# Gate and up of blocks 2 to 7 as seven products of 2x2 block matrices

## The reference

```python
x = fwht(x * SU_ug) / SCALE
x_up = x @ W_up.T * (Wscale_ug[:INTER] * SCALE)
x_gate = x @ W_gate.T * (Wscale_ug[INTER:] * SCALE)
x = jax.nn.silu(x_gate) * x_up
x = fwht(x * SU_dp) / SCALE
x = x @ W_down.T * (Wscale_dp * SCALE)
```

## Time and profile before

| | |
|---|---|
| median of 3 runs | 1306.21 us (1305.66 to 1310.3) |
| the profiled execution | 1306.45 us |
| its span, first to last instruction | 1304.6 us |
| mean granted TensorE clock | 0.979 of 2.4 GHz |
| PE busy / weight loads | 1226.0 us / 584.9 us |
| VectorE / ScalarE / GpSimd busy | 660.7 / 436.0 / 574.7 us |
| moved by DMA | 112.86 MB, mean 87 GB/s |

### The profile page before, as it was taken

One profiled execution on the slowest core, in us unless ns is written; L12 is line 12 of the kernel. 1 busy time (PEld: TensorE's weight loads), 2 busy tenths in 40 slices (PEclk: granted clock), 3 DMA queues, 4 the chain that ended last, 5 costly groups with the idle time before them and its releaser, 6 DMA issues.

```text
span 1304.6 us, 18006 instructions
## 1 busy us (share of the span) xinstructions
PE 1226.0 (94%) x6718; PEld 584.9 (45%) x6718; DVE 660.7 (51%) x1252; ACT 436.0 (33%) x828; POOL 574.7 (44%) x492
## 2 busy tenths in 40 slices
PE   7865879889999999999999999999999999999998
PEld 4552334334444444444444444444444444444444
DVE  2589599555564545544644545454554454451110
ACT  4874665521243023411432134302341143212210
POOL 1462487411575237531764166523753176311210
PEclk9987889999999999999999999999999999999999
DMA  9810144543452344333443345234433343120000
GB/s 322 309 33 1 33 73 87 107 97 65 113 106 59 95 104 106 65 81 90 109 93 73 87 107 106 51 96 104 106 65 81 93 109 82 33 73 9 1 1 32
DMA packets 230904, 112.86 MB, mean 87 GB/s; under 512 B 209400, under 2 KB 210736, under 8 KB 230320
## 3 DMA queue, kind: packets, MB, share of 16 engines
q1 hardware_dynamic: 219632, 77.52, 26.6%
q0 software_dynamic: 10240, 33.56, 9.3%
q10 hardware_dynamic: 960, 0.75, 0.2%
HBM read 52.82 MB, written 9.70 MB: 48 GB/s over the span
## 4 chain that ended last, share of the span: by engine, by line
PE 77%; DVE 9%; POOL 5%; ACT 4%; issue 3%; DMA 2%; SPq 0%; ACTq 0%; DVEq 0%; POOLq 0%
PE bank L1434 24%; PE bank L1435 24%; PE bank L1436 24%; DMA att<-ids_b 1%; POOL p L529 1%; PE bank L1610 1%; DVE wd L689 1%; POOL h_row L556 1%; POOL hid L580 1%; DVE a L1036 1%; PE bank L1429 1%; DVE h L677 1%; ACT sg L1147 1%; PE bank L1660 1%; PE bank L1499 1%
## 5 line engine op out<-in xcount | busy, mean ns | idle before, releaser
L1434 PE MATMUL bank<-xT,wgu 128*128 128x512 f16 x1024 | 391.4, 382 | 4.7 <-DVE a L1036 2.8
L1435 PE MATMUL bank<-xT,wgu 128*128 128x512 f16 x1024 | 391.3, 382 | 0.0
L1436 PE MATMUL bank<-xT,wgu 128*128 128x512 f16 x1024 | 391.0, 382 | 0.0
L580 POOL TENSOR_TENSOR hid<-a,hid 128x512 f16<-128x512 f32 x128 | 174.4, 1362 | 171.5 <-ACT hid L1150 171.3
L1036 DVE SCALAR_TENSOR_TENSOR a<-bank,kap,sg 128x512 f32<-128x512 f32 x128 | 96.0, 750 | 299.5 <-PE bank L1436 225.3
L1434 PE MATMUL bank<-wd,hid 128*128 128x512 f16 x512 | 195.2, 381 | 0.0
L1436 PE MATMUL bank<-wd,hid 128*128 128x512 f16 x512 | 195.1, 381 | 0.0
L1435 PE MATMUL bank<-wd,hid 128*128 128x512 f16 x512 | 195.1, 381 | 0.0
L1434 PEld LDWEIGHTS bank<-xT,wgu 128*128 128x128 f16 x1024 | 101.1, 99 | 125.1 <-issue 6.3
L1436 PEld LDWEIGHTS bank<-xT,wgu 128*128 128x128 f16 x1024 | 100.8, 98 | 123.0 <-issue 3.8
L1435 PEld LDWEIGHTS bank<-xT,wgu 128*128 128x128 f16 x1024 | 100.7, 98 | 118.7 <-issue 2.8
(11 more groups left out here) (223 smaller groups left out, 1470.0 us busy)
## 6 DMA issues: line engine op xcount, KB each, us to landing
out<-a SPq DMA_DIRECT2D x24, 256.0 KB
wgu<-in_L_ffn_W_gate SPq DMA_DIRECT2D x4, 1024.0 KB, 14.8
wgu<-in_L_ffn_W_up SPq DMA_DIRECT2D x4, 1024.0 KB, 15.0
wd<-in_L_ffn_W_down SPq DMA_DIRECT2D x4, 1024.0 KB, 15.8
out<-h_row SPq DMA_DIRECT2D x8, 256.0 KB
hid<-att_table,ids_p POOLq DMA_INDIRECT x72, 3.6
xT<-in_L_tok_proj_weight SPq DMA_DIRECT2D x1, 1024.0 KB, 8.6
p<-in_L_attn_Wq SPq DMA_DIRECT2D x1, 1024.0 KB, 12.0
```

What stands on the lines that cost most here:

```text
L580: nc.gpsimd.tensor_tensor(hid[:, 1, s, :], a32[:, :], hid[:, 0, s, :], ALU.subtract)\
L1434: mm(dst, w[0], v[0], start=first, stop=False)
L1435: mm(dst, w[0], v[1], start=False, stop=False)
L1436: return mm(dst, w[1], v[0], start=False, stop=final)
```

## The change

For one tile `f` gate and up together are a 2x2 block matrix (two halves of 256 rows of input each for gate and up) and the tokens a 2x2 block matrix too (input halves by halves of 256 tokens). Before, all eight block products are made. After, blocks 2 to 7 use seven (Winograd's form), each of six matmuls of 256 columns. Four of them need sums of weights (`S1` to `S4`) and sums of inputs (`T1` to `T4`).

The chain of partial results: bank `CHAIN[f % 2]` accumulates four products one after the other, and ScalarE copies the bank after each (`see`) before PE adds the next. `PAIR[f % 2]` takes the other three. VectorE adds copies and banks to gate and up (`upper`, `diagonal`); SiLU and the multiplication then read SBUF (`gated`) and run one slot later than the products.

The sums of weights are made during block 1 (`prep`: two additions of 512 and four of 256 columns on VectorE; a copy of 1,024 on ScalarE; a subtraction of 1,024 on GpSimd; 16 times), stored to DRAM (`products`, 917,504 bytes a tile) beside the plain quarters (`direct_store`, 32 DMAs). From then on six tiles are held in the SBUF room of `wgu`, and ScalarE issues a load of one tile per slot. The input's sums are made in slots 28 and 30 (`x_high_corner`, `x_low_corner`). The row copies wait for `stored` inside `head_high` now instead of at the loop's end. The diff's core:

```diff
 
+PREP_AT = (0, 2, 4, 5, 7, 8, 10, 11, 13, 14, 16, 18, 20, 22, 24, 26)
+FIRST_LOADS_AT = {21: (0,), 23: (3,), 28: (4, 5), 30: (1, 2)}
+HELD = 6
+HELD_AT = (18432, 11264, 14848, 22016, 25600, 29184)
+A11, A12, A22, S1, S2, S3, S4 = range(7)
...
                     fetch(b + 1, s)
-                    pair(b, s)
-            for s in range(SLOTS):
-                feed(NB - 1, s)
+                    product(b + 1, s)
+                    if s:
+                        feed(b, s - 1)
+                    attend(b + 1, s)
+            for s in range(1, SLOTS):
+                feed(NB - 1, s - 1)
 
...
+            def x_low_corner(n, m):
+                i, c = 4 * n + m, slice((m % 2) * P, (m % 2) * P + P)
+                mixed = PICK[1][:, :].rearrange("p (q k t) -> p q k t", q=2, k=2)
+                dve.wait_ge(S["xThi_done"], turned_high(n, m))
+                if m < 2:
+                    nc.vector.tensor_tensor(x_corner[:, 0:2, 1, :, c], mixed, x_corner[:, 0:2, 0, :, c], ALU.subtract)\
+                        .then_inc(S["xT_done"], 1)
+                    return
+                t = 6 * n + 3 * (m - 2) - 12
+                nc.vector.tensor_tensor(x_t[:, 0:256], PICK[1][:, 0:256], x_kept[m - 2][:, 0:256], ALU.subtract)\
+                    .then_inc(S["xt_done"], 1)
+                nc.vector.tensor_tensor(x_corner[:, B22, 1, :, c], mixed[:, 1, :, :], x_corner[:, B22, 0, :, c], ALU.subtract)
+                dve.wait_ge(S["xt_done"], t + 1)
+                nc.vector.tensor_tensor(x_t[:, 256:512], PICK[1][:, 256:512], x_t[:, 0:256], ALU.subtract)\
+                    .then_inc(S["xt_done"], 1)
+                dve.wait_ge(S["xt_done"], t + 2)
+                nc.vector.tensor_tensor(x_t[:, 512:1024].rearrange("p (a c) -> p a c", a=2),
+                                        x_kept[m - 2].rearrange("p (a c) -> p a c", a=2),
+                                        x_t[:, 256:512].rearrange("p (a c) -> p a c", a=1).broadcast_to([P, 2, 256]),
+                                        ALU.subtract).then_inc(S["xt_done"], 1)
+                dve.wait_ge(S["xThi_done"], turned_high(n, m) + 1)
+                nc.vector.tensor_tensor(x_sums[:, :, 1, :, c], x_t.rearrange("p (q k t) -> p q k t", q=4, k=2),
+                                        x_sums[:, :, 0, :, c], ALU.subtract).then_inc(S["xT_done"], 1)
...
+            def prep(f):
+                g, i = f // 4, f % 4
+                whole, sums, _ = prep_home(f)
+                if f == 0:
+                    dve.wait_ge(S["y_ready"], 4)
+                if f == 3:
+                    dve.wait_ge(S["direct_stored"], 512)
+                if f:
+                    dve.wait_ge(S["st_scaled"], staged_low(f - 1))
+                for j in range(2):
+                    w = wgu[:, 2 * g + j, i, :, :, :].rearrange("p l k f -> p l (k f)")
+                    last = nc.vector.tensor_tensor(whole[:, 512 * j:512 * j + 512], w[:, 0, :], w[:, 1, :], ALU.add)
+                link(last)
+                a11, a12, a21, a22 = [whole[:, 256 * j:256 * j + 256] for j in range(4)]
+                s1, s2, s3, s4 = [sums[:, 256 * j:256 * j + 256] for j in range(4)]
+                if f:
+                    dve.wait_ge(S["st_low"], staged_low(f - 1))
+                nc.vector.tensor_tensor(s3, a21, a11, ALU.subtract)
+                link(nc.vector.tensor_tensor(s1, a21, a22, ALU.add))
+                link(nc.vector.tensor_tensor(s2, s1, a11, ALU.subtract))
+                nc.vector.tensor_tensor(s4, a12, s2, ALU.subtract).then_inc(S["st_scaled"], 1)
...
+            def diagonal(b, f):
+                dve.wait_ge(S["chain_ready"], chain(b, f, 3))
+                dve.wait_ge(S["seen"], chain(b, f, 3))
+                nc.vector.tensor_tensor(corners[f % 2].rearrange("p (a c) -> p a c", a=4)[:, 0:4:3, :],
+                                        seen13[f % 2].rearrange("p (a c) -> p a c", a=2),
+                                        PAIR[f % 2][:, :].rearrange("p (a c) -> p a c", a=2), ALU.add).then_inc(S["corner_done"], 1)
+
+            def upper(b, f):
+                dve.wait_ge(S["p3_ready"], feeding(b, f) + 1)
+                nc.vector.tensor_tensor(corners[f % 2][:, 256:512], seen2[f % 2], PAIR[f % 2][:, 256:512], ALU.add)\
+                    .then_inc(S["corner_done"], 1)
+
+            def gated(b, f):
+                dve.wait_ge(S["silu_done"], FT * b + f + 1)
+                dve.wait_ge(S["seen"], chain(b, f, 4))
+                dve.wait_ge(S["corner_done"], 2 * FT * b + (2 * f - 4 * FT + 1))
+                dve.wait_ge(S["al_done"], FT * b + f - 1)
+                nc.vector.scalar_tensor_tensor(a_pair[f % 2], corners[f % 2][:, 512:1024], kap[:, f:f + 1], sg[:, :],
+                                               ALU.mult, ALU.mult).then_inc(S["a_done"], 1)
+
             def row_of(n, m):
...
+            def corner_slot(b, s, attending):
+                if 0 < s <= FT:
+                    upper(b, s - 1)
+                if attending:
                     if s == 0:
                         ids(b + 1)
                     else:
                         product(b + 1, s)
-                    feed(b, s, UP[s % 2])
+                if s < FT:
+                    diagonal(b, s)
+                if 0 < s <= FT:
+                    gated(b, s - 1)
+
...
 
+            def x_high_corner(n, m):
+                i, c = 4 * n + m, slice((m % 2) * P, (m % 2) * P + P)
+                mixed = PICK[1][:, :].rearrange("p (q k t) -> p q k t", q=2, k=2)
+                act.wait_ge(S["xhada_ready"], i + 1)
+                if m == 0 and isinstance(n, int):
+                    act.wait_ge(S["up_ready"], FT * n)
+                    act.wait_ge(S["sums_stored"], 160)
+                elif m == 0:
+                    act.wait_ge(S["p3_ready"], feeding(n, 0))
+                if m < 2:
+                    copy(x_corner[:, 0:2, 0, :, c], mixed)
+                    copy(x_kept[m], PICK[1][:, :]).then_inc(S["xThi_done"], 1)
+                    return
+                copy(x_corner[:, B22, 0, :, c], mixed[:, 1, :, :]).then_inc(S["xThi_done"], 1)
+                act.wait_ge(S["xt_done"], 6 * n + 3 * (m - 2) - 9)
+                copy(x_sums[:, :, 0, :, c], x_t.rearrange("p (q k t) -> p q k t", q=4, k=2)).then_inc(S["xThi_done"], 1)
...
+            def see(dst, b, f, number):
+                act.wait_ge(S["chain_ready"], chain(b, f, number))
+                copy(dst, CHAIN[f % 2][:, 0:256]).then_inc(S["seen"], 1)
+
+            def corner_slot(b, s, loading):
+                if s == 0:
+                    see(seen13[0][:, 0:256], b, 0, 1)
+                if s < FT:
+                    see(seen2[s % 2], b, s, 2)
+                    see(seen13[s % 2][:, 256:512], b, s, 3)
+                if 0 < s <= FT:
+                    f = s - 1
+                    act.wait_ge(S["corner_done"], 2 * FT * b + (2 * f - 4 * FT + 2))
+                    nc.scalar.activation(sg[:, :], corners[f % 2][:, 0:512], ACT.Silu, scale=sc[:, f:f + 1]).then_inc(S["silu_done"], 1)
+                    if f + HELD < FT:
+                        held_load(f % HELD, f + HELD)
+                    elif loading:
+                        held_load(f % HELD, f % HELD)
+                if s + 1 < FT:
+                    see(seen13[(s + 1) % 2][:, 0:256], b, s + 1, 1)
+                if s < FT:
+                    see(corners[s % 2][:, 512:768], b, s, 4)
+
+            def corner_high(b, s):
+                if 0 < s <= FT:
+                    f = s - 1
+                    if f == FT - 4 and not (isinstance(b, int) and b == NB - 1):
+                        for way in range(1, 5):
+                            act.wait_ge(S[f"pt_land{way}"], 48 * b)
+                    act.wait_ge(S["a_done"], FT * b + f + 1)
+                    copy(hid[:, 0, f, :], a_pair[f % 2]).then_inc(S["ah_done"], 1)
 
             def feed_high(b, s):
                 if s < FT:
...
-                    if s:
-                        product(b + 1, s)
-                    feed(b, s, GATE[s % 2])
-                    feed_high(b, s)
-                    if s == 0:
-                        product(b + 1, s)
+                    corner_slot(b, s, True)
+                    product(b + 1, s)
+                    corner_high(b, s)
                     attend(b + 1, s)
-                act.wait_ge(S["y_ready"], 4 * b + 4)
-                act.wait_ge(S["stored"], 64 * b + 64)
             for s in range(SLOTS):
-                feed(NB - 1, s, GATE[s % 2])
-                feed_high(NB - 1, s)
...
+            def quarter_product(dst, f, w, x, begin, final):
+                for k in range(2):
+                    last = split_mm(dst, [held[f % HELD][:, l, w, k, :] for l in range(2)], [XQ[x][:, l, k, :] for l in range(2)],
+                                    begin and k == 0, final and k == 1, skip_group_check=not begin)
+                return last
+
+            def p1(b, f):
+                j = feeding(b, f)
```

(76 more changed lines are left out.)

118 lines of the change are left out of this document (106 added, 12 removed).

## The result

The changed kernel takes 1555.99 us in the median of four runs (1543.34 to 1573.84), the one before 1308.26 beside it: ratio 1.172, 95% interval 1.162 to 1.183. The profiled execution took 1564.16 us, its span is 1562.4.

A forecast was written before the change was run, and what follows sets the result against it. PE streaming matmuls was taken as the bound from block 1 on. Blocks 2 to 6 +53.0, block 7 -6.0 and block 1 +15 gave +62.0 on 1306.45 us: 1368 us, range 1325 to 1410.

The forecast's parts named there:

- Fewer columns: PE's slot: 42 matmuls of 256 columns at 0.109 us take 4.58 us, 0.60 us less a slot.
- The rival of dear short matmuls: PE: short matmuls pay for their weight loads, 0.025 us each over 4,032, 1469 us in all; chance 0.02.
- Links and the shared way: Each slot: chain-bank copies add 0.16 us, VectorE and GpSimd excluding each other at SBUF 0.06; slot becomes 4.80 us.
- The sums over heads: Slots 4, 8, 12 with attention: PE stands 3.4 us behind ScalarE's copies; with VectorE's lag and clock 4.7, 14.1 a block.
- DMA, "Taken: 0": Added loads, 2.8 us each, one per slot, issued five slots ahead of use: costed at nothing.
- its upper end, 2 us at each of 15 head groups: Loads may delay the heads' transposes: at most 2 us at each waiting head group, 30 us.
- loads against transposes: Rival: loads delay the heads' transposes, +30 us, 1398 us in all; chance 0.13.
- Block 1, +15: Sixteen weight preparations: shared way into SBUF used 93 us where PE needs 80, plus 2.5; bounds 0 to 35, taken 15.
- Block 7, -6.0: Block without attention: 16 slots at -0.44 us, plus 1.0 for the input, gives -6.0 us.
- the +1.0 for the input: Block's start: the last input piece's chain takes 4.7 us against 2.6 and 1.3 us of cover; 1.0 us.
- VectorE waiting for a DMA at heads 4, 8 and 12: Sign that the prediction is wrong, looked for in the profile after; no size given.
- `diagonal` as PE's last releaser: Sign that the prediction is wrong: `diagonal` usually the last to release PE; no size given.

The follow-up runs named there:

- experiment 4: Changed kernel with the loop's loads issued on SyncE's queue, each behind the transposes of its slots, instead of on ScalarE's: 1451.21 us, ratio 1.110.
- experiment 5: Kernel with loads in line on SyncE's queue (1451 us), block 1's direct stores spread two a slot over slots 0 to 15: 1444.22 us, ratio 1.103.
- experiment 7: Kernel with loads in line on SyncE's queue (1451 us), sums of weights made ahead of `a` in block 1's slots 0 to 15: 1436.08 us, ratio 1.098.
- experiment 6: Kernel with loads in line on SyncE's queue, sums of weights left out, raw halves stored instead, first six loads issued later: 1424.45 us, ratio 1.087.

## Why the prediction was wrong

By its steps, with the profiled blocks; the forecast was +62 us, the profile has +258, and by the ratio it is +225. Two steps make the difference: the transfers taken at nothing, and block 1.

- **Fewer columns**: right. 42 matmuls take 4.58 us, 0.109 each. The rival of dear short matmuls would have made a slot 42 x 0.025 = 1.05 us longer; it did not.
- **Links and the shared way**: too dear. 4.80 us was forecast for the clean slot, 4.58 measured. There the covers of 0.76 us suffice, and `gated` finds its place. Some 3.5 us a block.
- **The sums over heads**: right in mechanism and place. 3.12 us idle (3.4 forecast), released by ScalarE's copy, low clock behind. Without the collision (experiment 4) all 15 waits are 3.0 to 3.1 us, and blocks 3 to 6 take 153.5 us, +12.3 where +10.6 was forecast. That this is near is in part luck: with a slot 0.2 us cheaper, the heads, slots 0 and 1 and the edges cost together about 5 us a block more than their terms.
- **DMA, "Taken: 0", "the cover is those five slots"**: this step failed. The cover is the loads' own; they were hardly late (PE waited 3.8 us for one, once). What they hit were the transposes, which have no such cover. The text saw that, but took it at nothing, and its upper end, 2 us at each of 15 head groups, has no row behind it. VectorE waited 9.3 us on average in 14 of 15. By the blocks it cost 891 - 776 = 115 us, by the ratios of experiment 4 81 us. The rival "loads against transposes" had the place and a quarter to somewhat over a third of the price.
- **Block 1, +15**: mis-sized, +81 measured. Its working counted the use of the way into SBUF (93 us against 80). The runs show 47.5 us for the sums, 14 for eight DMA issues in a row on ScalarE (5.3 to 7.2 us a slot), which the sum left out, and 20 unseparated; taken out in the other order it is 4 for the issues (experiment 5) and 57 for the sums (216.8 - 159.4). A tile's sums keep VectorE busy for 4.0 us, where 2.3 were reckoned. In the changed kernel's block 1 VectorE waits 44.4 us for SiLU and 21.6 for GpSimd's low halves, and ScalarE 21.6 for a store to land before it may reuse its home. Such waits in series had no term. Ahead of `a` the sums cost 8.2 us less (experiment 7); how the rest divides between waits and VectorE's longer work was not separated.
- **Block 7, -6.0**: -9.5; the links cost nothing (16 x -0.60 = -9.6), and of the +1.0 for the input nothing shows.

What was named as making the prediction wrong, VectorE waiting for a DMA at heads 4, 8 and 12, is what the profile showed. `diagonal` as PE's last releaser, also named, came with it: 117.1 us in 23 waits, 12.1 in 18 without the collision (experiment 4, from 552 to 1300 us).

## What to carry to other kernels

When a change adds transfers, ask of each transfer that is already there what its own slack is, above all transposes, and test the pair in flight together: an upper end of 30 us, set without such a test, was too low here by a factor of about three. If two kinds of DMA collide, try them in one queue, in the order of need, before cutting bytes. And for work that is added to a loop through three engines, write out the length of its chain, waits for landings and DMA issues included, and not only its share of an engine; block 1 suggests this, but its parts were not all separated.

## What the runs showed of the hardware

- DMA transposes on SyncE's queue and plain loads of 896 KB on ScalarE's, in flight together, hold each other up: average packets of 21 and 294 ns became 56 and 533 ns, and sixteen engines moved 125 GB/s while packet times added up to 99% of their time. The middle packet of either kind stayed as it was (18 and 276 ns, against 18 and 272); a few packets took up to 2.0 and 6.5 us. In one queue, a load behind its slots' transposes, the transposes landed in 3.3 us, as alone. Half the bytes a load cost nothing that shows; the same bytes in two DMAs, with packets at most half as long, cost less than in one. What happens inside the engines is open.
- A share of the DMA engines near 1 in this profile is a sum of packet times that overlap (1.81 in one stretch of 2 us), so it doesn't say that they are working at their rate.
- The kernel that has this collision scatters by 3% over six runs (1522.85 to 1573.84 us); the kernel before, beside it, by 0.4%.
- Eight DMA issues in a row hold ScalarE for 5.3 to 7.2 us, 0.66 to 0.9 us each; the stores of raw halves, two in a row (experiment 6), take 0.6 to 0.8 each, and a single load in a slot 0.34. Whether the row or the form of the transfer makes the difference was not tried.
